# Graph layers on one core: GpSimd waits on a nearer group (12, 5 or 7 places back, by pass) before it gathers

## The reference

```python
# layer 0: typed attention; layer 1: GAT; layer 2: graph convolution; layer 3: clipped attention
k_e, q_e, v_e = k[src], q[dst], v[src]                         # layer 0, relation by edge type
ex  = jnp.exp(a - amax[dst]);  att = ex / segment_sum(ex, dst)[dst]
agg = jax.ops.segment_sum(msg * att[..., None], dst, num_segments=n)
alpha = leaky_relu(a_src[src] + a_dst[dst])                    # layer 1, then the same softmax
agg = jax.ops.segment_sum(h[src], dst, num_segments=n)         # layer 2: no weights
# layer 3: exp(clip(q[dst].k[src], -5, 5)) weights v[src]
```

## Time and profile before

| | us |
|---|---|
| median of 3 runs (lowest to highest) | 12211.29 (12203.96 to 12215.69) |
| the profiled execution's own time | 12230.88 |
| its span | 12229.1 |
| busy: TensorE matmul / weight load | 7123.3 / 5769.1 |
| busy: VectorE / ScalarE / GpSimd | 4523.4 / 2930.1 / 6254.5 |

### The profile page before, as it was taken

One profiled execution on the slowest core, in us unless ns is written; L12 is line 12 of the kernel. 1 busy time (PEld: TensorE's weight loads), 2 busy tenths in 40 slices (PEclk: granted clock), 3 DMA queues, 4 the chain that ended last, 5 costly groups with the idle time before them and its releaser, 6 DMA issues. The chain is left out here.

```text
span 12229.1 us, 162378 instructions
## 1 busy us (share of the span) xinstructions
PE 7123.3 (58%) x41810; PEld 5769.1 (47%) x41811; DVE 4523.4 (37%) x12921; ACT 2930.1 (24%) x7688; POOL 6254.5 (51%) x6407
## 2 busy tenths in 40 slices
PE   5766666666665555555555433333335666666667
PEld 3555555555553444444444333222233555555555
DVE  4244444444454444444444411111113333333334
ACT  1233333333333333333333300000002211212112
POOL 1244444444543555555554466666663555555552
PEclk9866566665666555555555655556555665666667
DMA  3322222222221111111111122222222222222221
GB/s 116 134 69 66 68 70 67 69 70 68 69 61 41 38 37 38 38 37 38 37 38 36 42 46 46 46 46 47 46 46 64 76 76 74 77 77 76 75 76 49
DMA packets 379359, 730.33 MB, mean 60 GB/s; under 512 B 169738, under 2 KB 219201, under 8 KB 372838
## 3 DMA queue, kind: packets, MB, share of 16 engines
q0 software_dynamic: 251264, 621.88, 19.5%
q1 hardware_dynamic: 100474, 96.66, 2.4%
q10 hardware_dynamic: 27500, 10.39, 0.4%
HBM read 651.60 MB, written 76.88 MB: 60 GB/s over the span
## 5 line engine op out<-in xcount | busy, mean ns | idle before, releaser
L461 POOL DMA_INDIRECT edges_rows<-kv_typed,edges_idx_r x1568 | 1505.5, 960 | 1584.1 <-DVE edges_wv L781 1103.1
L461 POOL DMA_INDIRECT edges_rows<-gat_rows,edges_idx_r x1568 | 1523.3, 971 | 1421.3 <-DVE edges_wv L781 985.6
L461 POOL DMA_INDIRECT edges_rows<-kv_rows,edges_idx_r x1568 | 1516.6, 967 | 1237.5 <-DVE edges_wv L1145 775.7
L461 POOL DMA_INDIRECT edges_rows<-conv_rows,edges_idx_r x1568 | 1544.5, 985 | 777.0 <-issue 456.9
L609 PE MATMUL edges_ps_sum<-edges_wv,edges_pick 128*128 128x132 f32 x7040 | 1733.5, 417 | 96.5 <-issue 91.0
L985 PE MATMUL edges_ps_sum<-edges_rows,edges_pick 128*128 x3520 | 768.1, 356 | 1516.9 <-issue 1388.5
L609 PEld LDWEIGHTS edges_ps_sum<-edges_wv,edges_pick 128*128 128x128 f32 x7040 | 1466.0, 302 | 268.6 <-issue 246.8
L985 PEld LDWEIGHTS edges_ps_sum<-edges_rows,edges_pick 128*128 128x128 f32 x3520 | 648.9, 258 | 1636.1 <-issue 1634.5
L1083 PE MATMUL edges_ps_q<-q,edges_pick_t 128*128 x3520 | 799.1, 401 | 918.7 <-ACT edges_pick_t L1121 727.8
L1083 PEld LDWEIGHTS edges_ps_q<-q,edges_pick_t 128*128 128x128 f32 x3520 | 728.9, 305 | 968.5 <-issue 968.5
L591 PE MATMUL edges_ps_q<-q,edges_pick_t 128*128 x3520 | 821.9, 409 | 563.9 <-ACT edges_pick_t L696 429.5
(11 more groups left out here) (344 smaller groups left out, 11299.7 us busy)
## 6 DMA issues: line engine op xcount, KB each, us to landing
kv_typed<-l0pre_out SPq DMA_DIRECT2D x49, 1024.0 KB
edges_rows<-kv_typed,edges_idx_r POOLq DMA_INDIRECT x1568
edges_rows<-gat_rows,edges_idx_r POOLq DMA_INDIRECT x1568
edges_rows<-conv_rows,edges_idx_r POOLq DMA_INDIRECT x1568
edges_rows<-kv_rows,edges_idx_r POOLq DMA_INDIRECT x1568
edges_feat_r<-visit_features ACTq DMA_DIRECT2D x660, 10.0 KB
kv_rows<-l3pre_kv SPq DMA_DIRECT2D x7, 896.0 KB, 4.0
edges_flag_r<-visit_flags ACTq DMA_DIRECT2D x220, 16.0 KB
```

Of the source, the lines that this page charges most:

```text
L461: pool.indirect_dma_start(rows[:, k, g * width:(g + 1) * width], None, table, bass.IndirectOffsetOnAxis(ap=idx_r[:, k, g:g + 1], axis=0)). ...
```

## The change

`fetch` gets a number `ahead`. GpSimd waits, before group j, for the last visit of group j-`ahead` in place of group j-14. The number is 12 in passes 0 and 1, 5 in pass 2, and 7 in pass 3. The ring keeps its 14 slots, and the indices and `rows_ready` work as before. As waits now begin before group 14, the words of the table are read once more in the first groups, where the place j-`ahead` may be below zero.

```diff
-def fetch(nc, pool, res, rows, table, width, idx_r, idx_in, rows_in, rows_ready, used, slot_free):
+def fetch(nc, pool, ahead, res, rows, table, width, idx_r, idx_in, rows_in, rows_ready, used, slot_free):
...
             if known(j, SLOTS):
-                visits[:] = words(pool, res, 3, j - SLOTS, HALF)
-        if known(j, SLOTS):
+                visits[:] = words(pool, res, 3, j - ahead, HALF)
+            elif known(j + HALF - 1, ahead):
+                short = max(ahead - j, 0)
+                visits[:] = [None] * short + list(words(pool, res, 3, j - ahead + short, HALF - short))
+        if known(j, ahead):
             pool.wait_ge(used, at_least_one(pool, visits[k % HALF], NV))
...
# softmax_pass
-                fetch(nc, pool, res, rows, table, width, ...
+                fetch(nc, pool, 12, res, rows, table, width, ...
# conv_pass
-                fetch(nc, pool, res, rows, table, aw, ...
+                fetch(nc, pool, 5, res, rows, table, aw, ...
# clipped_pass
-                fetch(nc, pool, res, rows, table, width, ...
+                fetch(nc, pool, 7, res, rows, table, width, ...
```

More of the change, by code:

```diff
@@ L533, in _ @@
             def _(pool):
-                fetch(nc, pool, res, rows, table, width, idx_r, idx_in, rows_in, rows_ready, wv_done, slot_free)
+                fetch(nc, pool, 12, res, rows, table, width, idx_r, idx_in, rows_in, rows_ready, wv_done, slot_free)
             @block.tensor
@@ L967, in _ @@
             def _(pool):
-                fetch(nc, pool, res, rows, table, aw, idx_r, idx_in, rows_in, rows_ready, sum_done, slot_free)
+                fetch(nc, pool, 5, res, rows, table, aw, idx_r, idx_in, rows_in, rows_ready, sum_done, slot_free)
             @block.tensor
@@ L1047, in _ @@
             def _(pool):
-                fetch(nc, pool, res, rows, table, width, idx_r, idx_in, rows_in, rows_ready, wv_done, slot_free)
+                fetch(nc, pool, 7, res, rows, table, width, idx_r, idx_in, rows_in, rows_ready, wv_done, slot_free)
             @block.tensor
```

## The result

| | us |
|---|---|
| kernel before, beside it | 12204.29 (12179.65 to 12226.39, 15 runs) |
| changed kernel | 12235.73 (12220.45 to 12263.13, 15 runs) |
| ratio | 1.0027, 95% interval 1.0018 to 1.0036 |
| profiled execution of the changed kernel: own time, span | 12246.44, 12244.6 |

The change costs 31 us (22 to 44 by the interval). The forecast was +62: the sign is right, the size is twice too large.

What follows compares the result with a forecast made beforehand. Gather bursts were taken to delay TensorE, binding pass 2 by GpSimd's issue and pauses, the other passes by the rows' users. Terms -4 - 4 - 16 + 86 = +62 us on 12211.3 gave 12273 us, range 12135 to 12390 (8 in 10).

Steps and rivals of the forecast that it cites:

- What bounds the kernel: Long gather bursts delay TensorE's counts and use up GpSimd's lead; pass 2 bound by GpSimd, others by the rows' users.
- Passes 0 and 1, start and end (-10, +6): First burst two groups shorter, -10 us; two more groups used up at the end, +6; net -4 each pass.
- Pass 3, start and end (-37, +22): Third weighing 37 us sooner; at the end 7 groups lose the free pace, +22; net taken as -16 us.
- The middle of passes 0, 1 and 3 (nothing): The nearer limit only shifts GpSimd against the users; burst length stays, added waits are hidden: 0 us.
- the cover of 20 us: Passes 0 and 3, middle: rows still come about 20 us before they are needed, so added waits stay hidden.
- rival C: Rows come late in passes 0, 1 or 3, 250 us on top: 12520 us; chance 0.05.
- Pass 2 (+86): GpSimd's rests in pass 2: 67 bursts of 30 us with 5.0 us pauses, 335 us less 249 before: +86 us.
- rival A: Pass 2 pauses shrink with the burst, to 2.8 us: -85 us, 12126 us; chance 0.25.
- the likeliest case: The forecast that pass 2 loses, spanning 12235 (pause of 4.4 us) to 12398 us (+187); chance 0.48.
- B's 12187: Only starts and ends count, pass 2 keeps its 249 us of pauses: 12187 us; chance 0.16.
- D: TensorE is slow without GpSimd, pass 2 waits 22 us in each of 43 cycles: +690 us, 12877; chance 0.02.
- E: The new wait never binds, nothing moves: 12211 us; chance 0.04.

Runs made afterwards that it cites:

- the session with three leads: Pass 2 leads 14, 5, 3 timed together: drained kernel (own rests in passes 0, 1, 3) 12826.61 us, changed kernel 12046.01, lead 3 alone 12072.92; kernel before 12027.23.
- 14 everywhere: Changed code with all leads set to 14, the same waits as the kernel before: ratio 1.0003 against it, in the 9300 us surroundings.
- the last experiment: Changed kernel with 14 in pass 2 (12, 12 and 7 elsewhere), against the kernel before: 12229.94 us, ratio 1.0005.

## Why the prediction came out as it did

- *What bounds the kernel.* Right for these surroundings: late counts, bursts, and a free stretch after each rest. Only "holds TensorE up" was too narrow: in the burst shown above TensorE works on time and its count is late. In other stretches, as in the earlier trace rows and in 119 of the 440 visits of pass 2 before, its records come slowly too; why was not found. (The prediction's "one matmul in 2.8 us" is one record, which is half a matmul.)
- *Passes 0 and 1, start and end (-10, +6).* Right for pass 0, and for the start of pass 1. GpSimd's start in pass 0 (timeline), and the first work of ScalarE behind the burst:

```profile
535.62 0.98 POOL L464 DMA_INDIRECT edges_rows<-kv_typed,edges_idx_r  x1 [44.63 <-DMA edges_idx_r<-typed_sources]
...
594.40 0.94 POOL L464 DMA_INDIRECT edges_rows<-kv_typed,edges_idx_r  x1 [0.30 <-issue]
624.24 0.94 POOL L464 DMA_INDIRECT edges_rows<-kv_typed,edges_idx_r  x1 [28.89 <-DVE edges_wv L784]
```

```profile
601.83 0.60 ACT L699 ACTIVATE edges_pick_t<-edges_ps_pick_t 128x512 f32<-128x512 f32 x1 [28.53 <-remote]
```

  The first wait stands after 12 groups and ends 88.6 us after the first gather, not 97.7: -9. At the end the tail behind the last gather shrinks from 42.2 to 31.4 us while GpSimd ends 2 groups of 7.8 us later: 15.7 - 10.8 = +5. In pass 1, which the prediction took to be the same, the first weighing comes 10 us sooner too, but the tail stays (41.9 and 41.3 us), so the end costs +14 and not +6.
- *Pass 3, start and end (-37, +22).* Right at the start, and too dear at the end. GpSimd, then the weighings 0 to 2 on VectorE:

```profile
9380.28 0.95 POOL L464 DMA_INDIRECT edges_rows<-kv_rows,edges_idx_r  x1 [25.80 <-DMA edges_idx_r<-sources]
...
9419.03 0.94 POOL L464 DMA_INDIRECT edges_rows<-kv_rows,edges_idx_r  x1 [0.30 <-issue]
9427.59 0.95 POOL L464 DMA_INDIRECT edges_rows<-kv_rows,edges_idx_r  x1 [7.62 <-DVE edges_wv L1148]
```

```profile
9402.98 0.68 DVE L1148 TENSOR_TENSOR edges_wv<-edges_rows,edges_wv 128x512 f32<-128x512 f32 x1
...
9426.12 0.69 DVE L1148 TENSOR_TENSOR edges_wv<-edges_rows,edges_wv 128x512 f32<-128x512 f32 x1
...
9429.53 0.69 DVE L1148 TENSOR_TENSOR edges_wv<-edges_rows,edges_wv 128x512 f32<-128x512 f32 x1
```

  The third weighing starts 49.3 us after the first gather, not 90.1: -41. At the end the tail goes from 51.9 to 16.2 us for 7 groups of 7.0: 49 - 36 = +13.
- *The middle of passes 0, 1 and 3 (nothing): a step that failed.* Rows are never late once a pass has started: from the fifth visit on those of a multiplication are announced at least 10 us ahead in pass 0, 22 in pass 1 and 6 in pass 3, and 25, 40 and 25 us at the median, so the cover of 20 us was right and rival C is out. Its sign, a pass 0 longer by more than 10 us, did come (+26, and +15 with 14 in pass 2), so that sign did not mean late rows. "Nothing" was a little too good: the mean time to a group (groups 20 to 370) of pass 0 is 7.886 us against 7.829, and 7.737 against 7.686 in the two kernels of one session with 12 and 14: +0.05 both times, +20 us over the pass. In pass 1 it is 7.517 against 7.551 and 7.355 against 7.411: -12 and -20 us. In pass 3 it is 7.016 against 7.018 and 6.870 against 6.787: 0 and +29 us. The forecast for the three passes was -24 us and the timed kernels give +6 (-6 to +20). Pass 0's middle and pass 1's end are where the profiles have it; the profiled executions differ from their medians by up to 34 us, so they can't place it better, and why pass 0 takes longer to a group stays open.
- *Pass 2 (+86): the step that failed most.* The failed term is "67 x 5.0 = 335", and in it the price, "I take 5.0 us, nearer to pass 3". No row had shown a rest at such bursts. Measured are 71 rests of 4.0 us on average, 286 us in all, with bursts of 27.6 us on average: number and length nearly as forecast, the price a quarter too high, and +41 us in place of +86. (The bursts are uneven: 52 long ones of 36.6 us with 4.6 us behind each, and 20 short ones with 2.5.) A rest of 4.0 us is even below the 4.1 from which rival A would win by the prediction's own sum; the kernel lost all the same, as there were 71 rests and not 67, and the -24 did not come. And a term was missing: the gathers themselves got faster, 971 ns on average against 985, 1568 x 14 ns = -22 us (in the session with three leads 971 against 980, -13 us). With -7 in the short gaps and -1 at the end that is +10 in the profile. The timed kernels give 25. The upper end of the likeliest case, 12398, leaves out the -24; with it it is 12374.
- *What of it was luck.* +62 was the sum of -24 and +86; measured are +6 and +25. The two terms are off by 30 and 61 us in opposite directions, and half of the larger error was cancelled by the other.
- *Rivals.* A's idea (shorter rests) is true and its price of 2.8 us is not; at a lead of 3 a rest was still 3.4 us. B's 12187 lies below all runs. D is out: there is no rest of 22 us in pass 2, the longest is 6.3. E is out: the first waits come after 12 groups in passes 0 and 1 and after 8 in pass 3.
- *The rule weighed.* The Trainium skill, "SBUF — State Buffer", section "Who interferes with whom": a DMA never contends with a compute engine. In the 9300 us surroundings the traces agree (0.15 us from matmul to addition beside unbroken gathers). In the 12000 us ones they don't fit it, if it is read as more than a rule on SBUF's ports: beside the same gathers an addition of pass 2 starts up to 72 us after its matmul, and rests of 2.9 us between the groups bring the longest lateness of a TensorE count from 33 us down to 4.3 in pass 0. Whether a port plays any part in this is not shown.

## What to carry to other kernels

When a consumer's count comes late beside a busy issuer, look at what ends the wait in time, not at the releaser named: in pass 2 of the kernel before the waits ended 1.1 to 9.5 us after GpSimd had stopped, 5.4 on average. A limit on the lead cuts such bursts only where it binds, and pays with more rests; a short rest placed by the issuer itself after every second group gained 4.5% where a nearer limit lost 0.3%, both in the 12000 us surroundings. And measure the kernel before anew each time: an effect that hangs on the surroundings may be wholly absent the next time, and a remedy for it may then be a loss.

## What was not expected of the hardware

- One program has two times, 9301 to 9313 and 12027 to 12234 us, with nothing between. It does not seem to be a property of a chip: the results of 14 everywhere (kernel before at 9301 us) and of the last experiment (12224 us) name the same chip number. The granted clock does not explain it: 0.64 against 0.60 on average, and in pass 1, 2082 against 2977 us long, it is 0.50 in both (in pass 0 it is 0.73 against 0.61). Stretches of the passes 0 and 1 with 14 everywhere at 9305 us, for comparison with the earlier trace rows:

```profile
534.90:2581.40 2046.50, 1766.00 (x12967) 1488.48 (x12967) 1308.73 (x3846) 1059.37 (x2640) 1541.40 (x1568) 0.73 0.36 103
2734.70:4816.70 2082.00, 1623.18 (x12967) 1343.15 (x12968) 1283.81 (x4511) 958.44 (x2640) 1581.12 (x1568) 0.50 0.24 53
```

- VectorE, ScalarE and GpSimd are busy for nearly the same time in both (4487, 3002 and 6361 us with 14 everywhere; 4523, 2930 and 6255 before); what differs is their idle time. What decides between the two surroundings stays open.
- The last of a group's four gathers has its last recorded landing 1.4 to 1.8 us (median, by pass) after its issue has ended, both in the kernel before in the 12000 us surroundings and with 14 everywhere in the 9300 us ones: the rows come at their time, the counts of TensorE don't.
